# Attention with a modulated norm on one Trainium2 core: where the softmax division is done, and in which order the steps run

## The reference

```python
scale, shift = split(emb @ W_emb + b_emb)
xn = rms_norm(x, g_norm) * (1.0 + scale) + shift
q, k, v = heads(xn @ W_qkv)
q = rms_norm(q, g_q); k = rms_norm(k, g_k)
attn = softmax(einsum('bhqd,bhkd->bhqk', q, k) * d ** -0.5)
o = merge(einsum('bhqk,bhkd->bhqd', attn, v))
return x + (o + o @ W_out)
```

## Time and profile before

| | us |
|---|---|
| median of 3 runs | 2257.38 |
| lowest and highest run | 2257.04, 2260.83 |
| span of the profiled execution, first to last instruction | 2255.9 |
| TensorE busy | 2176.2 (96%) |
| VectorE busy | 1748.6 (78%) |
| ScalarE busy | 1411.7 (63%) |
| GpSimd busy | 931.4 (41%) |

### The profile page before, as it was taken

How to read it: one execution, slowest core, us unless ns; L and a number is a source line. 1 busy time by engine, 2 the same in 40 slices (tenths; PEclk the granted TensorE clock), 3 DMA queues, 4 the chain that set the end, 5 groups by cost and what they waited for, 6 DMA issues and landing times.

```text
span 2255.9 us, 39472 instructions
## 1 busy us (share of the span) xinstructions
PE 2176.2 (96%) x13392; PEld 1992.2 (88%) x13392; DVE 1748.6 (78%) x3511; ACT 1411.7 (63%) x3077; POOL 931.4 (41%) x1241
## 2 busy tenths in 40 slices
PE   7788789999999999999999999999999999999999
PEld 3676678999999999999999999999999999999989
DVE  4799988678985699767986689857897569876786
ACT  4577766467854577546864578646775458754663
POOL 3866674235532345223541246312553325422330
PEclk9899999999999999999999999999999999999999
DMA  7655464777556765568555675566654775656842
GB/s 299 238 212 226 188 224 147 269 269 254 192 187 241 271 218 196 175 236 289 207 202 197 230 285 192 189 238 242 230 205 165 254 281 199 203 192 227 294 157 103
DMA packets 141528, 497.55 MB, mean 221 GB/s; under 512 B 14864, under 2 KB 61968, under 8 KB 140304
## 3 DMA queue, kind: packets, MB, share of 16 engines
q1 hardware_dynamic: 141328, 495.03, 61.7%
HBM read 425.77 MB, written 69.21 MB: 219 GB/s over the span
## 4 chain that ended last, share of the span: by engine, by line
PE 77%; DVE 11%; issue 4%; DMA 4%; ACT 3%; POOL 1%; SPq 0%; DVEq 0%; ACTq 0%
PE proj_bank L597 16%; PE proj_bank L599 16%; PE proj_bank L598 16%; PE flip_bank L721 8%; PE pv_bank L732 5%; PE pv_bank L733 5%; PE score_bank L713 4%; PE score_bank L714 4%; DMA w_ring<-qkv_store 2%; DVE neg_max L1069 2%; DVE probs L1075 2%; PE score_bank L686 2%; DVE pt_lo L1079 1%; ACT pt_hi L866 1%; ACT probs L860 1%
## 5 line engine op out<-in xcount | busy, mean ns | idle before, releaser
L597 PE MATMUL proj_bank<-w_ring,xa_hi 128*128 128x384 f32 x1792 | 626.5, 350 | 21.0 <-DVE xa_lo L1058 7.6
L599 PE MATMUL proj_bank<-w_ring,xa_lo 128*128 128x384 f32 x1792 | 606.4, 338 | 0.0
L598 PE MATMUL proj_bank<-w_ring,xa_hi 128*128 128x384 f32 x1792 | 605.7, 338 | 0.0
L860 ACT ACTIVATE probs<-score_bank,neg_max 128x512 f32<-128x512 f32 x512 | 352.1, 690 | 250.0 <-DVE neg_max L1069 242.6
L866 ACT CAST pt_hi<-flip_bank 128x512 fp32r<-128x512 f32 x512 | 296.3, 586 | 235.7 <-PE flip_bank L721 148.3
L1079 DVE TENSOR_TENSOR pt_lo<-flip_bank,pt_hi 128x512 fp32r<-128x512 f32 x512 | 346.6, 686 | 117.0 <-ACT pt_hi L866 111.6
L1069 DVE TENSOR_REDUCE neg_max<-score_bank 128x1 f32<-128x512 f32 x512 | 341.4, 684 | 75.0 <-PE score_bank L714 71.7
L597 PEld LDWEIGHTS proj_bank<-w_ring,xa_hi 128*128 128x128 f32 x1792 | 340.6, 190 | 40.8 <-issue 13.5
L598 PEld LDWEIGHTS proj_bank<-w_ring,xa_hi 128*128 128x128 f32 x1792 | 341.3, 190 | 9.6
L599 PEld LDWEIGHTS proj_bank<-w_ring,xa_lo 128*128 128x128 f32 x1792 | 339.6, 190 | 0.0
L721 PE MATMUL flip_bank<-ident,probs 128*128 128x128 f32 x2048 | 294.3, 274 | 14.5 <-DVE probs L1075 7.3
(11 more groups left out here) (91 smaller groups left out, 3855.3 us busy)
## 6 DMA issues: line engine op xcount, KB each, us to landing
w_ring<-qkv_store SPq DMA_DIRECT2D x392, 768.0 KB, 5.7
w_ring<-wo_store SPq DMA_DIRECT2D x108, 512.0 KB, 4.7
qkv_store<-w_ring SPq DMA_DIRECT2D x56, 768.0 KB, 4.9
x_tile<-in_x SPq DMA_DIRECT2D x36, 512.0 KB, 7.8
w_raw<-in_x SPq DMA_DIRECT2D x112, 128.0 KB, 6.4
out<-w_raw SPq DMA_DIRECT2D x112, 128.0 KB, 1.9
...
```

The costliest lines, as they stand in the source:

```text
L597: nc.tensor.matmul(dst, a_hi, w[:, 0, :], start=start, stop=False, skip_group_check=shared)
L598: nc.tensor.matmul(dst, a_hi, w[:, 1, :], start=False, stop=False, skip_group_check=shared)
L599: return nc.tensor.matmul(dst, a_lo, w[:, 0, :], start=False, stop=stop, skip_group_check=shared)
L860: nc.scalar.activation(probs[h][:, i, :], score_bank[n % 2][:, :], ACT.Exp, bias=neg_max[:, n:n + 1], accum_out=row_sum[:, n:n + 1]).then_ ...
```

## The change

The probabilities are no longer divided by their row sum before they are turned. They go through F and W undivided, and the finished output of a pair is multiplied by the inverse sums instead.

- N on VectorE becomes one reciprocal of all eight row sums of a pair (128x8), after the pair's last exponential. `row_sum` and `row_inv` become two buffers each, by `it % 2`.
- In the output the query rows lie along the free axis, so the inverses are needed as rows, the same for all 64 partitions of a head. New steps on SyncE bring them there: `store_inv` (N0) writes the 128x8 tile to device memory as one row of 512 per head, in pieces of four bytes; `load_inv` (N1), two loads, waits for that store and reads each row back into 64 partitions of `o_lo`, which is free until Q writes the pair's low half. It carries the waits that Q had (P63 of the batch before; the raw weights).
- A new step N on GpSimd waits for both loads and both output sums, and multiplies `o_pair` by `o_lo` in place. Q on ScalarE waits for that.
- F waits for the exponentials of its head. ScalarE's first exponential of a pair waits for the reciprocal of the pair two before; VectorE's reciprocal waits for the store of the pair two before.
- The step lists of all engines in all three tables are new. The same steps stand in them, apart from N; among others, SyncE's x and residual loads, which stood in one block ahead of `4W4`, now stand between the weight loads.

The diff, its step lists cut to the places named in this document:

```diff
 BODY = {
     "TensorE": """
-        4C0 4C1 4C2 2W0 2W1 4C3 4C4 2F4 2W2 2F5 2W3 4C5 2W4 2F6 2F7 2W5 4C6 3F0 2W6 3S6 3F1 2W7 3S7 4C7 3F2 3W0 3W1 3F3
...
-        P47 P48 11T0 P49 P50 10F1 11T1 P51 P52 P53 10F2 P54 P55 P56 10F3 11S0 P57 11S1 P58 P59 P60 11S2 P61 11S3 P62 P63
-        11S4 11S5""".split(),
+        4C0 4C1 4C2 4C3 4C4 2W0 2W1 4C5 2W2 2F4 4C6 2F5 2W3 2F6 2W4 4C7 2W5 2F7 2W6 3F0 4C8 2W7 4C9 3F1 3S6 4C10
...
+        P48 P49 P50 11T0 P51 P52 11T1 P53 10F1 P54 P55 10F2 P56 9W7 P57 P58 11S0 P59 P60 P61 10F3 11S1 P62 11S2
+        P63 11S3 11S4 11S5""".split(),
     "ScalarE": """
...
-        11S1 11S2 11S3 8Q0 9O0 12E0 9O1 10F2 9Q0 10F3 12E1""".split(),
+        11D2 10S3 10S4 10S5 9F7 10F0 11D3 10S6 10S7 11T0 11T1 10F1 11S0 10V1 11S1 11S2 11S3 8Q0 12E0 9O0 12E1
+        9O1 10F2 10F3 9Q0""".split(),
     "GpSimd": """
-        0Q0 1Q0 3V0 +A0 3V1 4D0 2Q0 4D1 +A1 +A2 +A3 4M0 4M1 4D2 4M2 4D3 4V0 4M3 3Q0 4V1 5D0 5M0 5D1 5D2 5D3 5M1 5M2 5M3
+        0Q0 1N0 1Q0 3V0 3V1 +A0 4D0 2N0 +A1 4M0 4D1 +A2 2Q0 4M1 4D2 4M2 4D3 4M3 +A3 5D0 5M0 5D1 5D2 5M1 3N0 5M2
...
+        10M2 10M3 11D0 11M0 11D1 10V0 11M1 11D2 11M2 11D3 11M3 8N0 10V1""".split(),
     "SyncE": """
-        -O15 E0 +X0 +X1 +X2 +X3 E1 E2 E3 E4 E5 E6 E7 E8 E9 E10 E11 4W4 4W5 4W6 4W7 4W8 4W9 4W10 4W11 4W12 4W13 6W0 6W1
...
-        W0 W1 W2 W3 W4 W5 W6 O0 E12 O1 E13 O2 W7 E14 10W0 10W1 O3 O4 E15 O5 O6 10W2 10W3 O7 10W4 10W5 10W6 10W7 10W8
-        10W9 10W10 10W11 10W12 10W13 W8 W9 W10 W11 W12 W13 W14 O8 O9 O10 W15 12W0 12W1 O11 O12 O13 O14 12W2 12W3""".split(),
+        4W4 +X0 -O15 +X1 +X2 E0 4W5 +X3 4W6 4W7 4W8 E1 4W9 4W10 4W11 E2 4W12 E3 3N0 4W13 6W0 3N1 6W1 6W2 E4 6W3
+        6W4 6W5 6W6 6W7 4N0 4N1 6W8 6W9 6W10 6W11 6W12 E5 6W13 8W0 8W1 8W2 E6 8W3 E7 E8 8W4 8W5 5N0 8W6 5N1 6N0
+        8W7 8W8 8W9 6N1 8W10 8W11 8W12 8W13 W0 7N0 7N1 W1 W2 W3 W4 W5 E9 W6 W7 E10 10W0 E11 O0 10W1 8N0 O1 10W2
+        10W3 E12 O2 O3 10W4 O4 10W5 E13 10W6 10W7 E14 10W8 10W9 E15 10W10 10W11 10W12 10W13 W8 O5 W9 W10 O6 W11
+        W12 O7 O8 9N0 W13 W14 O9 W15 12W0 O10 12W1 12W2 10N0 O11 O12 8N1 9N1 O13 O14 12W3 10N1""".split(),
 }
...
+    inv_store = nc.dram_tensor("inv_store", (B * PAIRS, 2, TT, P), F32, kind="Internal").ap()
...
-        row_sum = sb("row_sum", [P, 8])
-        row_inv = sb("row_inv", [P, 8])
+        row_sum = [sb(f"row_sum{i}", [P, 8]) for i in range(2)]
+        row_inv = [sb(f"row_inv{i}", [P, 8]) for i in range(2)]
...
                     elif kind == "F":
                         flip_wait(pe, u)
                         if i == 0:
-                            pe.wait_ge(probs_ready, it * 8 + (4 * h + 4))
+                            pe.wait_ge(exp_done, it * 8 + (4 * h + 4 + CREDIT))
...
+                        if n == 0:
+                            wait_past(act, inv_done, it - 1)
                         nc.scalar.activation(probs[h][:, i, :], score_bank[n % 2][:, :], ACT.Exp,
                                              bias=neg_max[:, n:n + 1],
-                                             accum_out=row_sum[:, n:n + 1]).then_inc(exp_done, 1)
+                                             accum_out=row_sum[it % 2][:, n:n + 1]).then_inc(exp_done, 1)
...
                     elif kind == "Q":
-                        act.wait_ge(o_sum_done, it * 2 + (2 + CREDIT))
+                        act.wait_ge(o_scaled, it + 1)
...
                     elif kind == "N":
-                        dve.wait_ge(exp_done, it * 8 + (n + 1 + CREDIT))
-                        nc.vector.reciprocal(row_inv[:, n:n + 1], row_sum[:, n:n + 1]).then_inc(inv_done, 1)
-                        dve.wait_ge(inv_done, it * 8 + (n + 1))
-                        nc.vector.tensor_scalar(probs[h][:, i, :], probs[h][:, i, :], row_inv[:, n:n + 1], None,
-                                                ALU.mult).then_inc(probs_ready, 1)
+                        dve.wait_ge(exp_done, it * 8 + (8 + CREDIT))
+                        if it >= 2:
+                            dve.wait_ge(inv_stored[it % 2], 16 * (it // 2))
+                        nc.vector.reciprocal(row_inv[it % 2][:, :], row_sum[it % 2][:, :]).then_inc(inv_done, 1)
...
+                    elif kind == "N":
+                        pool.wait_ge(inv_loaded[it % 4], 32 * (it // 4 + 1))
+                        pool.wait_ge(o_sum_done, it * 2 + (2 + CREDIT))
+                        nc.gpsimd.tensor_tensor(o_pair[:, :], o_pair[:, :], f32(o_lo[:, p % PAIRS, :]),
+                                                ALU.mult).then_inc(o_scaled, 1)
...
+            def store_inv(it):
+                sp.wait_ge(inv_done, it + 1)
+                sp.dma_start(inv_store[it].rearrange("h i p -> p (h i)"), row_inv[it % 2][:, :],
+                             allow_slow_non_contiguous=True).then_inc(inv_stored[it % 2], 16)
+
+            def load_inv(it, head):
...
+                if head == 0:
+                    sp.wait_ge(inv_stored[it % 2], 16 * (it // 2 + 1))
+                    if it >= PAIRS:
+                        sp.wait_ge(proj_done, TILES[("P", it // PAIRS - 1, NOUT - 1)] + TT)
+                    if it in (5, 6, 7):
+                        for done in w_lo_even, w_lo_odd:
+                            sp.wait_ge(done, PAIRS // 2 * COUPLE)
+                src = inv_store[it, head].rearrange("i p -> (i p)").unsqueeze(0).to_broadcast([DH, T])
+                sp.dma_start(f32(o_lo[rows(head), it % PAIRS, :]), src).then_inc(inv_loaded[it % 4], 16)
```

In HEAD's list of VectorE, what stands ahead of Y2:

```diff
-        X0 X4 Y0 0J0 X2 0J1 0J2 Y1 Y4 G0 G1 G2 G3 X6 G4 G5 Y5 0D0 0L4 G6 0J3 0L5 0L6 Y3 Y2 0J4 G7 0L7 0D1 0E4 0E5 0J5
+        X0 X4 Y0 X2 0J0 0J1 Y1 Y4 G0 X6 G1 Y5 G2 Y3 G3 G4 0L4 G5 G6 0L5 G7 Y2 0L6 0D0 0J2 0D1 0L7 0L8 0E4 0J3
```

More of the change, by code:

```diff
@@ new lines @@
+    "SyncE": """
+        0H0 0H1 0H2 0H3 0H4 0H5 0H6 0H7 0H8 0H9 0H10 2G0 2G1 2G2 0H11 0H12 2G3 0H13 +X0 2H0 2H1 +X1 2H2 0N0 0N1
+        2H3 2H4 2H5 2H6 2H7 2H8 2H9 1N0 2H10 4G0 4G1 4G2 1N1 2H11 2H12 4G3 2H13 4H0 4H1 +X2 +X3 4H2 4H3 2N0 4H4
+        2N1 4H5 4H6 4H7 4H8 4H9 4H10 6G0 6G1 6G2 4H11 4H12 6G3 4H13 3N0 3N1 6H0 6H1 6H2 6H3 6H4 6H5 4N0 6H6 6H7
+        6H8 6H9 4N1 6H10 G0 5N0 G1 6H11 6H12 8W0 6H13 8W1 5N1 8W2 8W3 8W4 8W5 E0 8W6 8W7 E1 E2 8W8 6N0 8W9 8W10
+        8W11 6N1 7N0 8W12 8W13 7N1 H0 G4 H1 H2 E3 G5 O0 H3 O1 H4 O2 G8 E4 E5 H5 H6 O3 G9 H7 O4 10W0 E6 E7 10W1
+        10W2 10W3 10W4 10W5 O5 10W6 10W7 10W8 10W9 E8 10W10 10W11 O6 10W12 E9 10W13 E10 H8 G12 H9 H10 G13 O7 8N0
+        H11 E11 H12 O8 H13 O9 H14 E12 O10 E13 12W0 12W1 E14 H15 9N0 O11 O12 12W2 10N0 E15 8N1 9N1 10N1 O13 12W3
+        O14""".split(),
@@ new lines @@
+        P5 P6 6S4 6S5 6F0 P8 P9 6S6 P10 6F1 P12 P13 P14 6F2 6F3 6S7 P16 6W0 7T0 P17 7T1 P18 P20 P21 P22 P24 6W1
+        6F4 6W2 P25 7S0 6F5 6W3 7S1 P26 P28 7S2 6W4 6F6 P29 6W5 7S3 6F7 P30 P32 6W6 7S4 7F0 6W7 7F1 7S5 P33 7S6
+        P34 7S7 P36 7W0 7F2 P37 P38 P40 P41 P42 7F3 7W1 P44 P45 7F4 7W2 7W3 7F5 P46 P48 7W4 7F6 7F7 7W5 P49 P50
+        7W6 7W7 P52 P53 P54 P56 P57 P58 P60 P61 P62 P3 P7 P11 P15 P19 P23 P27 P31 P35 P39 P43 P47 P51 P55 P59
+        P63""".split(),
+    "ScalarE": """
+        2F4 2F5 2F6 3S4 2F7 4E2 3V0 3F0 4D0 4E3 2O0 3V1 4D1 3S5 3S6 2O1 3F1 3S7 3F2 3F3 3F4 3F5 4D2 2Q0 4D3 3F6
+        3O0 5D0 5D1 4T0 3F7 4T1 5D2 4V0 3O1 6E0 5D3 4S0 4V1 4S1 4S2 6E1 4S3 6E2 4S4 4F0 4S5 4F1 4S6 6E3 4S7 5T0
+        4F2 4F3 5T1 4F4 3Q0 4F5 5V0 6D0 5S0 4F6 4F7 5S1 6D1 5S2 5V1 5S3 5F0 4O0 5S4 4O1 5S5 5F1 5F2 5S6 5F3 4Q0
+        5S7 6D2 6D3 5F4 5O0 5F5 5F6 5F7 7D0 6T0 5O1 6T1 5Q0 7D1 6S0 6S1 6S2 6S3 6V0 6S4 6V1 7D2 6F0 7D3 6F1 6S5
+        6S6 6S7 7T0 6F2 7T1 6F3 6F4 7S0 7V0 6F5 6O0 7S1 6F6 7S2 6F7 7S3 7S4 7S5 7F0 7S6 7F1 6O1 7V1 7S7 7F2 7F3
+        7F4 6Q0 7F5 7O0 7F6 7F7 7O1 7Q0""".split(),
@@ new lines @@
+    "VectorE": """
+        2F4 2F5 2F6 2F7 2O0 3F0 3S6 4E4 2O1 4D0 3F1 4E5 4E6 3S7 3F2 4E7 3F3 4D1 3F4 4E8 4D2 3F5 4E9 4D3 3F6 3N0
+        4E10 4E11 3F7 4E12 4T0 4T1 5D0 4E13 5D1 5D2 4S0 5D3 4S1 4S2 4S3 3O0 4S4 4S5 4F0 4S6 4S7 4F1 3O1 4F2 4F3
+        5T0 5T1 4F4 5S0 4F5 4N0 5S1 4F6 4F7 5S2 5S3 6E4 6D0 5S4 6E5 5F0 6E6 5S5 4O0 5F1 5S6 5F2 6E7 6D1 4O1 5S7
+        5F3 6E8 5N0 6E9 6D2 5F4 6D3 5F5 5O0 5F6 6E10 5F7 6T0 7D0 6E11 5O1 6E12 6T1 6E13 6S0 6S1 6S2 6S3 K0 7D1
+        6S4 7D2 K1 6S5 7D3 6F0 6S6 K2 6F1 K3 6S7 K4 6F2 7T0 7T1 6F3 K5 7S0 6N0 6F4 K6 6F5 7S1 6F6 7S2 7S3 6F7 K7
+        7S4 6O0 7S5 7S6 7F0 K8 7S7 K9 7N0 7F1 7F2 7F3 6O1 K10 7F4 K11 7F5 7F6 7F7 7O0 K12 7O1 K13 K14 K15 R0 R1
+        R2 R3 R4 R5 R6 R7 R8 R9 R10 R11 R12 R13 R14 R15""".split(),
@@ L199 @@
     "GpSimd": """
[L200 to L201 removed]
+        0Q0 1N0 1Q0 3V0 3V1 4D0 4D1 2N0 4M0 4M1 4D2 4M2 2Q0 4D3 4M3 4V0 5D0 4V1 5M0 5D1 5D2 5D3 5M1 5M2 5M3 3N0
+        5V0 5V1 3Q0 6D0 6M0 4N0 6D1 4Q0 6M1 6D2 6M2 6D3 6M3 7D0 5N0 5Q0 6V0 7D1 7M0 7D2 6V1 7M1 7D3 7M2 7M3 7V0
+        7V1 6N0 6Q0 7N0 7Q0""".split(),
@@ L206 @@
+        W11 W15 O0 O1 O2 O3 O4 O5 O6 O7 O8 O9 O10 O11 O12 O13 O14 O15""".split(),
 }
@@ L467, in cond_attention @@
         inv_done = sem("inv_done")
-        probs_ready = sem("probs_ready")
```

(8 more changed lines are left out.)

254 lines of the change are left out of this document (114 added, 140 removed).

## The result

The changed kernel takes 2474.28 us (median of 4 runs, 2468.02 to 2483.13) against 2257.95 us for the kernel before on the same chip: 1.0961 times as long, 95% interval 1.0938 to 1.0985. The forecast was 2225 us. Its profiled run took 2468.02 us with a span of 2466.2 us.

The account below looks back on a forecast made before the run. It took TensorE as the bound in later batches and VectorE in the first batch's stage. Gains of 34 and 2 us less 4 made 32 us off 2255.9, so 2225 us as median; range 2204 to 2252.

Parts of the forecast that it names:

- The store: SyncE's store of a pair's inverses: landing about 2.5 us, between 1.9 and 11.5; cost of standing on SyncE taken as 0.
- my upper end: Upper bound for the store's landing: 11.5 us, as for the small constants that stood behind other loads.
- The slower rival: At batch boundaries the two loads land in 11.5 us, E0 is 9.3 us late seven times: 2286 us; chance 0.12.
- First batch, 34 us: First batch's stage: gain of 34 us from divisions and reciprocals leaving VectorE, between 6.9 and 51 us.
- Start, 2 us: Ahead of the first batch's stage: new order shortens TensorE's wait for an operand's low half, gain 2 us (0 to 7.6).
- Body, 0: Six later batches and the end: gain taken as 0, between 0 and 10 us, since TensorE idles only 1.4 us there.
- Boundary, 0.5 us each: Seven batch boundaries: loads, multiply and Q start only after P63, losing 0.5 us each, 4 us in all (0 to 29).
- Sum: Whole kernel: 34 + 2 - 4 = 32 us less than the profiled 2255.9, forecast 2225 us as median.
- the store's sign: Sign in the profile after that the forecast is wrong through the stores: weight loads gain share of the chain.
- The 11 us: First batch: GpSimd's eight added multiplies may each block a VectorE step for 1.41 us, giving back 11 us: 2236.

Follow-up runs that it names:

- e1: Changed kernel with each pair's 4 KB store in 128 pieces of 32 bytes instead of 1024 of 4 bytes, values at wrong columns; 2234.69 us.
- e2: Changed kernel with its 4-byte-piece store, but loads read the row stored two pairs earlier, so none waits for its own pair's store; 2443.18 us.
- s4: The repaired version, correct output: changed kernel with VectorE turning the inverses in 32 x 32 blocks, stored in 128 pieces of 128 bytes; 2235.87 us.
- e4: Changed kernel without store or loads of inverses; GpSimd multiplies by a vector resident in SBUF; new step orders kept; 2215.40 us.
- o1: Changed kernel without store or loads of inverses, multiplying by a resident vector, but in the step orders of the kernel before; 2246.24 us.
- s5: s4 with the inverses of each batch's first pair, from the third batch on, loaded into two tiles taken from the output ring; 2234.23 us.
- s1: Changed kernel, all pairs loading the first two pairs' inverses (wide-piece stores); later stores, unread, are 1024 pieces of 4 bytes, 512 bytes apart; 2231.70 us.

## Why the prediction was wrong, point by point

- **The store, the step that failed.** "From below: 1.9 us to landing", "from above: 11.5 us", "I take about 2.5"; and for what it costs on SyncE, "I take 0". SyncE's wait for it measured 7.9 us on average and 12.4 at most. The larger fault lay in what I asked: I priced the store as a delay of its own, "a few us of standing cost nothing where the ring is full". Of the 240 us between the changed kernel and e1, standing is 31; some 208 stay when no load waits for its pair's store (e2), and come from other transfers held up beside it, a term the sum didn't have. No row of before shows many pieces of a few bytes written side by side into device memory, and `b_col`, my upper end, is a load, with pieces of 64 bytes.
- **The slower rival had the wrong place.** I put it at the boundary, by a long landing of the loads, and priced it at 2286 us, 188 below what was measured; that the way was slower does not bear it out. The mechanism exists: in the changed kernel's chain (start, us) the load of a first pair lands after 10.53 us and E0 comes late. But it is the store's crowding that makes loads land so late (median 11.9 us in e2, where no load waits for its pair's store, 3.2 in s4), and TensorE's direct waits there are 35.6 us in 5 (`u_part`, above).

```profile
775.65 0.45 SPq L1344
...
776.14 10.53 DMA o_lo<-inv_store
...
786.74 1.26 POOL o_pair L1196
```

- **First batch, 34 us.** Without transfers 41.6, with the repaired store 38.7: the size was fair. In the changed kernel itself only 6 are left, the store crowding there too. The reason was right only in part: I gave the whole to divisions leaving the chain, but in the old orders only 14.3 us come. VectorE kept 212 us of work, not 202: I took the busy times of two lines from a busy time in which instructions that overlap count once. In the trace of before the stage's VectorE busy time without these two lines is about 208 us, where I had 201.
- **Start, 2 us:** 3 to 4 (97.0 in e4 and 97.9 in the changed kernel against 100.9), from the orders, since o1 has 100.3. **Body, 0:** right without transfers (265.3 to 267.1 us a batch).
- **Boundary, 0.5 us each.** With the repaired store the later batches are about 2 us longer than without transfers (s4 against e4), so 4 us in all was low by some 10. Whether they are lost at the boundary isn't settled: s5 eased it there and won nothing.
- **Sum.** 32 us were forecast; the repaired version's span is 24.5 us under that of before (2231.4 against 2255.9), inside the range. That is another kernel's time and does not save the forecast; it says that the other terms were near, apart from some 10 us in the later batches. The bytes added are 17.0 MB (514.57 - 497.55), not 16.6. The text did name the store's sign, "if weight loads gain share of the chain (stores)": they went to 12%, from 2%.
- **The rules of the Trainium skill.** By the Trainium skill ("SBUF — State Buffer", "Who interferes with whom") GpSimd's multiplies would hold up VectorE's instructions with two inputs in SBUF. The 11 us that I took for it do not show: VectorE's 44 steps on `w_ring`, part of the weight split, fill 29.7 us of the first stage before, 28.5 in o1 and 34.3 in e4, and both of these have all eight multiplies. Of the rule of the Trainium skill on a non-contiguous last dimension ("DMA: Bandwidth & Descriptors", "Rules for kernel authors") I wrote that by it the stores would be slow, and gave that no chance of its own. The trace agrees that each element is a packet (packets under 512 bytes rose from 14864 to 83472), but s1 has nearly as many (81680) and they cost nothing: it is how they lie that decides. The Trainium skill, on the same page ("DMA: Bandwidth & Descriptors", "Specifications"), puts the least transfer for full rate at 512 bytes. No run here measures the rate of a store by itself; pieces of 32 bytes, and of 4 bytes at 64 apart, showed no cost in the kernel's time.
